# Who issues the zero fills: thirty DMAs moved from SyncE's queue to GpSimd's

## The reference

```python
h = relu(layernorm(x)); x = x + gcn(h, W, b, gamma, beta, src, dst)
h = relu(layernorm(x)); x = x + attention(h, edge_index, edge_attr, Wq, Wk, Wv, We, ...)
h = relu(layernorm(x)); x = x + gat2(gat1(h))
h = relu(layernorm(x)); x = x + sage2(sage1(h))

# attention, and in the same pattern the two GAT layers, for each edge src -> dst
logits = sum(q[dst] * (k[src] + e)) / sqrt(C)          # GAT: leaky_relu(el[src] + er[dst])
ex     = exp(logits - segment_max(logits, dst)[dst])
out    = segment_sum(ex / segment_sum(ex, dst)[dst] * (v[src] + e), dst)
```

## Time and profile before

| | us |
|---|---|
| median of three runs | 2882.3 |
| lowest and highest run | 2879.76, 2882.7 |
| span of the profiled execution, first to last instruction | 3131.6 |

### The profile page before, as it was taken

One profiled execution on the slowest core, in us unless ns is written; L12 is line 12 of the kernel. 1 busy time (PEld: TensorE's weight loads), 2 busy tenths in 40 slices (PEclk: granted clock), 3 DMA queues, 4 the chain that ended last, 5 costly groups with the idle time before them and its releaser, 6 DMA issues.

```text
span 3131.6 us, 33483 instructions
## 1 busy us (share of the span) xinstructions
PE 2171.3 (69%) x10859; PEld 1508.0 (48%) x10859; DVE 1424.4 (45%) x3094; ACT 961.2 (31%) x2148; POOL 1362.2 (43%) x1417
## 2 busy tenths in 40 slices
PE   4899999468777777545666676682443443489998
PEld 3566667257666666332333333352333332356666
DVE  6766663646665655633444444332222222431414
ACT  3523321422233332553433443241222222220302
POOL 3000000666666663466666665257666666300000
PEclk9777778767888887768888888695555555599999
DMA  9479862277777885125666676314444554456361
GB/s 217 126 268 317 280 210 73 85 198 227 223 226 224 231 226 146 26 62 168 215 210 218 196 216 202 115 44 100 117 116 110 120 125 105 142 168 197 116 202 48
DMA packets 518583, 517.97 MB, mean 165 GB/s; under 512 B 153344, under 2 KB 463763, under 8 KB 517227
## 3 DMA queue, kind: packets, MB, share of 16 engines
q1 hardware_dynamic: 310349, 267.63, 28.1%
q0 software_dynamic: 50528, 115.22, 14.6%
q10 hardware_dynamic: 157534, 132.98, 13.7%
HBM read 301.53 MB, written 227.32 MB: 169 GB/s over the span
## 4 chain that ended last, share of the span: by engine, by line
PE 38%; another core or an unknown queue 15%; issue 14%; POOL 11%; DVE 9%; DMA 7%; ACT 6%; ACTq 1%; SPq 0%; POOLq 0%; DVEq 0%
PE ps L1577 9%; POOL arena L1047 9%; PE ps L1480 6%; PE ps L1470 6%; PE ps L1670 5%; ACT arena L1078 4%; DMA ends_gat<-arena 3%; DMA ends_attn<-arena 2%; PE ps L1559 2%; PE ps L1610 1%; PE ps L1620 1%; DVE arena L1988 1%; PE ps L1848 1%; DVE arena L2338 1%
## 5 line engine op out<-in xcount | busy, mean ns | idle before, releaser
L1078 ACT ACTIVATE arena<-ps 128x774 f32<-128x774 f32 (+8 forms) x689 | 496.8, 729 | 1548.0 <-remote 674.3
L1047 POOL DMA_INDIRECT arena<-t_gat,src_i x784 | 741.5, 946 | 373.1 <-issue 221.0
L1670 PE MATMUL ps<-arena 128*128 128x136 f32 (+2 forms) x2352 | 703.7, 460 | 283.0 <-ACT arena L1078 153.1
L1670 PEld LDWEIGHTS ps<-arena 128*128 128x128 f32 x2352 | 468.7, 265 | 449.4 <-issue 240.3
L1047 POOL DMA_INDIRECT arena<-t_attn,src_i x392 | 378.4, 965 | 211.9 <-issue 106.6
L1577 PE MATMUL ps<-arena 128*128 128x384 bf16 x1850 | 305.4, 329 | 34.3 <-issue 25.2
L1577 PEld LDWEIGHTS ps<-arena 128*128 128x128 bf16 x1850 | 182.0, 99 | 157.5 <-issue 40.2
L2338 DVE TENSOR_TENSOR arena<-arena,ps 128x1536 f32<-128x1536 f32 (+1 forms) x196 | 230.2, 1216 | 53.8 <-ACT arena L1217 35.6
L2322 DVE TENSOR_TENSOR dif<-logit,ps 128x64 f32<-128x64 f32 (+2 forms) x147 | 27.5, 187 | 459.3 <-remote 340.4
L1628 PE MATMUL ps<-ident,logit 128*64 128x128 f32 (+2 forms) x147 | 49.3, 335 | 265.5 <-issue 161.1
L1480 PE MATMUL ps<-arena 128*128 128x100 bf16 x1176 | 222.6, 364 | 10.9 <-DVE arena L2118 10.6
(11 more groups left out here) (321 smaller groups left out, 2833.7 us busy)
## 6 DMA issues: line engine op xcount, KB each, us to landing
ends_gat<-arena ACTq DMA_DIRECT2D x98, 774.0 KB
arena<-adj_hbm SPq DMA_DIRECT2D x90, 640.0 KB
same_b<-same_hbm SPq DMA_DIRECT2D x294, 128.0 KB
adj_hbm<-arena SPq DMA_DIRECT2D x9, 3200.0 KB, 12.4
ends_attn<-arena ACTq DMA_DIRECT2D x98, 272.0 KB
ends_gat<-arena ACTq DMA_DIRECT2D x98, 258.0 KB
arena<-edst SPq DMA_DIRECT2D x98, 256.0 KB, 4.8
starts_q<-zrow SPq DMA_DIRECT2D x28, 896.0 KB, 6.8
```

The lines of the kernel that those rows point to most:

```text
L1047: g.indirect_dma_start(out=row_b[:, n % RB, k, 0:row_tab[p].shape[1]], out_offset=None, in_=row_tab[p], in_offset=bass.IndirectOffsetOnAxi ...
L1078: return a.activation(o, i, ACT.Copy)
L1670: i = mm(o, same_f[:, g % RB, k, :], msg[:, g % 4, k * W:(k + 1) * W], start=True, stop=True)
```

## The change

The function that issues a fill moves from SP's program to POOL's, and so do the 30 calls. On POOL they stand behind the 20 step gathers and the memset of the ones column (L983 before), ahead of the waits for the parameters and for the fills themselves. The transfers, their sizes and the semaphore stay the same. Nothing is added that waits: the fills have no wait ahead of them on POOL.

```diff
@@ SP, the loop over the groups
-            def zeros(t, parts, at, wide):
-                n = EP * t.shape[1] // P // parts
-                flat = t[0:EP, :].rearrange("(b p e) c -> b p (e c)", b=parts, p=P)
-                sp.dma_start(flat[at].rearrange("p (a n) -> p a n", n=wide),
-                             zrow[:, 0:wide].rearrange("p (a n) -> p a n", a=1).to_broadcast([P, n // wide, wide]))\
-                  .then_inc(s_zero, 16)
...
                 store_same(g)
                 if g + UNROLL < NG:
                     load_dst_row(g + UNROLL)
-                if g >= 10 and g % 2 == 0 and g // 2 - 5 < ZERO_PARTS:
-                    zeros(starts["attn"], ZERO_PARTS, g // 2 - 5, 256)
-                elif g in (71, 73):
-                    p = ("gat1", "gat2")[(g - 71) // 2]
-                    zeros(starts[p], 1, 0, 392)
@@ POOL, behind the step gathers
             g.memset(xs0[:, :, 3 * D:XW], 1.0).then_inc(s_ones, 1)
+            def zeros(t, parts, at, wide):
+                n = EP * t.shape[1] // P // parts
+                flat = t[0:EP, :].rearrange("(b p e) c -> b p (e c)", b=parts, p=P)
+                pool.dma_start(flat[at].rearrange("p (a n) -> p a n", n=wide),
+                             zrow[:, 0:wide].rearrange("p (a n) -> p a n", a=1).to_broadcast([P, n // wide, wide]))\
+                  .then_inc(s_zero, 16)
+
+            for part_at in range(ZERO_PARTS):
+                zeros(starts["attn"], ZERO_PARTS, part_at, 256)
+            for p in ("gat1", "gat2"):
+                zeros(starts[p], 1, 0, 392)
```

## The result

The changed kernel is slower: 2933.27 us, the median of four runs (2930.69 to 2937.68), against 2882.5 us for the kernel before in the same job (four runs, 2879.76 to 2892.17). The ratio is 1.0167, with a 95% interval of 1.0143 to 1.0192. That is 50.8 us lost where 0.7 us was forecast; the time lies above the range of the prediction (2874 to 2915 us). The profiled execution of the changed kernel has a span of 2936.0 us.

What follows compares the result with a forecast made beforehand. The prediction took PE to bound the GCN loop; gain 0 and cost 0, the added work being covered, left the median at 2882.3 us, written as 2883 us, with an 8-in-10 range of 2874 to 2915 us.

Steps and rivals of the forecast that it cites:

- What bounds the loop: GCN loop: PE alone bounds it, three periods taking 64.65 us with fills and 64.87 us without.
- the gain of 0: GCN loop: taking 30 DMA issues off SP wins 0, at most the 6.2 us that PE waited there.
- rival 3: GCN loop: without the fills' 26.7 MB every PE wait goes, 6.2 us, 2876 us; chance 0.11 with anything else faster.
- The price of a fill: POOL's issuing after the memset: 6.6 us a fill, counted by pieces, so fills run from 57 to about 255 us.
- the bound that goes by the gather: POOL's issuing: a fill costs what a step gather costs, 1.25 us, 37 us for all 30.
- the point from which it decides: End of preparation: at 4.1 us a fill the copy ends after about 118 us and the parameter loads' cover is gone.
- three bounds: POOL's total for the 30 fills: 37 us by gather cost, 198 us by pieces, 392 us by bytes.
- What the fills leave to the copy: DMA engines from 57 us: fills take 38%, the edge-feature copy keeps 62%, and the four destination loads are out at 94 us.
- an end at 103 us: Edge-feature copy under fast fills: with packets alike it keeps half of the engines, ends at 103 us and costs nothing.
- The cover of 14 us: SP before the loop: parameter loads end at 118 us, 14 us before the first store at 131.82 us, so cost 0.
- Rival 1: End of preparation: fills issued well under 4 us each starve the copy, tiles wait 27 and 37 us; 2914 us, chance 0.28.
- Rival 2: DVE and PE while POOL issues: unnamed waits of 0.5 us per us of issuing, up to 99 us, 2981 us; chance 0.08.

Runs made afterwards that it cites:

- the kernel paced with 9 writes: Changed kernel with nine small memsets on POOL, each waited for, behind each of the 28 part fills: 2891.53 us, ratio 1.0022.
- the second profile of before: The kernel before, unchanged, profiled once more because the first profile's span was 249.3 us above the runs: 2880.76 us, span 2879.1 us.

## Why the prediction was wrong

**What bounds the loop: right.** PE bounds it, and its periods are 65.09 us with and without fills in it. So the gain of 0 was right too, and rival 3 (the loop gains 6.2 us) is refuted.

**The price of a fill: the step that failed.** I took "6.6 us a fill, since each piece needs a descriptor". The trace has 0.95 us, below the 1.25 us of the bound that goes by the gather, and smaller pieces show 0.2 ns for each piece. I had the point from which it decides, 4.1 us, and stood on the wrong side of it; I chose the middle of three bounds that were a factor of ten apart, by an argument about descriptors that no row bore. The rest of the sum nearly held near the assumed price: in the kernel paced with 9 writes, a fill every 5.7 us, the four loads are out at 89.5 us, against 94 us predicted, and the runs lose 6 us. The Trainium skill's page "DMA: Bandwidth & Descriptors" says in "Anatomy of one DMA — SWDGE (gpsimd) path" that descriptor generation is small and that many descriptors can be emitted before the cost shows up; these two numbers bear it out.

**What the fills leave to the copy: wrong in the same direction.** From fills spread over 198 us I had left the copy 62% of the engines and its end at 94 us. The queues of the changed kernel show the share (packets, MB, share of the 16 engines): q1 from 40 to 60 us, before the fills; q0 and q1 from 70 to 110 us; q1 from 110 to 122 us; q1 from 135 to 145 us.

```profile
q1 hardware_dynamic: 17808, 4.56, 100.3%
```

```profile
q0 software_dynamic: 3639, 13.89, 94.4%
q1 hardware_dynamic: 3412, 0.87, 9.6%
```

```profile
q1 hardware_dynamic: 6515, 1.66, 61.2%
```

```profile
q1 hardware_dynamic: 52, 0.01, 0.6%
```

SP's queue q1 falls from 4.56 MB in 20 us to 0.87 MB in 40, from 228 to 22 KB/us. The two queues move nearly the same number of packets, but a packet of a fill is 13.89 MB / 3639 = 3.8 KB and one of the copy 0.87 MB / 3412 = 256 bytes, a row of 64 floats. The copy does not stay shut out until the fills are over, though. The first 17 fills have all but drained before POOL issues the other eleven at 116.34 us, and from 110 to 122 us the copy gets 1.66 MB through. Then the second lot comes. From 135 to 145 us q0 moves 3.30 MB and q1 only 52 packets, 5.2 a us. From 70 to 110 us it moved 85 a us, and a sixteenth of that is 5.3, as if the rows of a single one of the 16 engines were left; the trace does not name the engine. SP is free of the first load at 151.2 us (31.96 + 119.28), as the second lot of fills ends: q0 moves 0.10 MB from 152 to 154 us and nothing in the 16 us after. By this reading the last 30 us of SP's wait go to a small rest of the copy that met the second lot. In the kernel with half of the fills, which has no second lot, SP is free at 114.6 us. The turns by whole packets of the section "Queues, rings and completion order" of that page of the Trainium skill agree with the packet counts; the sum that I drew from it, an end at 103 us, needed packets alike, and they are not.

**The cover of 14 us: not there.** It was read against a first store at 131.82 us. On the axis of an execution as long as the runs, the last parameter store ends at 101.36 us and the first store of the loop stands at 112.71 us, 11 us apart, less than the 14 us by which I had the parameters move. The fifth tile at 129.61 us would still have held that. It did not hold what came: SP was free of the parameters 76 us later (177.46 us against 101.36).

**Rival 1: the mechanism, with the size too small.** Its places came out close: the first tile at 158 us (156.05 measured), the fifth at 186 us (182.12). That is partly luck: it had the copy shut out until 133 us and alone for 23 us after, while in the trace nearly all of the copy is through by 122 us and a rest of it holds SP until the second lot of fills is over, in an execution that is 6.2 us late before the fills begin. Its price was too small, since the times at which the two tiles were needed were 112.0 and 129.6 us. Against those the rival's own numbers give 158 - 112 = 46 us and 186 - 129.6 = 56 us in place of 27 and 37; measured are 50.8 us in the runs and 45.6 us in the loop of the two profiles. It had a chance of 0.28, and the range ended at 2915 us for it. With need times from an execution as long as the runs its time would have come out at 2882 + 46 to 56, 2928 to 2938 us.

**Rival 2 (signals come late while POOL issues): not seen.** The unnamed waits of the earlier trace rows appear neither after nor in the second profile of before, though POOL issues in both. They were seen in the long execution alone, and the profiler as such does not add them. The paced kernels, in the first of which POOL issues fills from 60.83 to 219.56 us, bound such a cost at 6 us, where I had allowed 99.

## What to carry to other kernels

A DMA that is moved to an engine with nothing ahead of it starts at that engine's issue rate; ask what the queue's owner did to space it out before, and what transfer is in flight at the place to which it goes. Where a long transfer of small packets meets a burst of large ones, look at who stands behind the long one in its queue: with the flood kept, moving that one copy to another queue took the loss from 50.8 us to within the runs' scatter, and pacing the fills took away 45 us of it. And when a profiled execution is far longer than the runs, as here by 249.3 us, its places in time are not to be used as need times before a second profile has the span of the runs.

## What the runs showed of the hardware

- GpSimd's issue of a direct DMA took 0.95 us for 896 pieces (changed kernel) and 1.53 us for 3584 (smaller pieces); an estimate from these two is about 0.8 us and 0.2 ns a piece.
- GpSimd ran ahead of the transfers by about 15,000 pieces and then stopped: after 17 fills of 896 (15,232 pieces, 37.17 us in the changed kernel, 51.80 us with the fills behind the loads), and after every 4 of 3584 (14,336 pieces, some 17 to 27 us each time). In the changed kernel it went on only when these had drained: the queue of the fills moved 0.01 MB from 116 to 118 us, and POOL issued again at 116.34 us.
- In the changed kernel a queue of 256-byte packets beside one of 3.8 KB packets got 22 KB/us instead of 228, a tenth. The packets of the fills were of 3.8 KB with pieces of 1 KB and with pieces of 256 bytes.
- SP hung in an issue until the earlier copy of 12,480 KB in its own queue had all but drained: 51.94 us in the second profile of before, 121.23 us under the flood, 63.89 us at the first store with the copy behind the loads, 1.77 us with the copy in ACT's queue.
- SP's parameter issues took 23 us in the second profile of before, 33 us beside fills paced with 9 writes and 45 us beside the fills in smaller pieces.
